# A backward-branch hint on TensorE's inner loop of a GRU recurrence

## The chip, the cores and the metric

The kernel runs on 1 core of one Trainium2 chip. The metric is the device time of one execution in microseconds (us): the median of the runs shown. TensorE is called PE, its weight loads PEld, VectorE DVE, ScalarE ACT, GpSimd POOL and SyncE SP. Each engine has a sequencer that takes instructions in program order, does register work, waits and branches itself, and hands the rest to the engine; the profile writes the sequencer of PE as PEq or PEldq. L340 is line 340 of the kernel.

## The reference

The whole program is one transformer-like layer over x of shape (4, 512, 512): a GRU over the time axis, a causal differential attention with a frequency filter, a second attention, and a mixture of 64 experts with a shared one. Only the GRU bears on the change. With D = 512, B = 4 and T = 512 steps:

```python
def cell(h, x):
    gi = x @ W_ih + b_ih
    gh = h @ W_hh + b_hh
    i_r, i_z, i_n = jnp.split(gi, 3, axis=-1)
    h_r, h_z, h_n = jnp.split(gh, 3, axis=-1)
    r = jax.nn.sigmoid(i_r + h_r)
    z = jax.nn.sigmoid(i_z + h_z)
    n = jnp.tanh(i_n + r * h_n)
    h_new = (1.0 - z) * n + z * h
    return (h_new, h_new)
```

Each step needs the h of the step before, so 512 steps follow one another whatever else is free. All numbers are float32.

## The kernel before

`gru_stage` does the 512 steps. W_hh lies in the tile `ahead`, cut into 4 row chunks (c) and 4 column chunks (j). On PE one step is two functions.

`add_z_input(s, par)` (L296 to L305) waits for the pick of the step from POOL and for two DVE transposes of earlier steps, and then writes the z gate's input into PSUM, 4 products of 32 columns at L300 and 4 of 96 at L304.

`step(s, par)` multiplies h by W_hh, always at L311 in the helper `part`. It waits for the first quarter of h (`h_ready[0]`), multiplies it for the r and z columns (`gru_prz`) and the n columns (`gru_pn`), waits for the rest of h (`h_ready[1]`), and multiplies the other three quarters for `gru_prz`, `gru_pn` and last `gru_pz`. DVE transposes the results (L410, L415, L423), ACT applies sigmoid and tanh, and DVE forms the new h in two scans at L429, which release the next step's `h_ready[0]` and `h_ready[1]`.

For the first 480 steps PE also prepares the recurrence inputs 32 steps ahead: between `add_z_input` and `step` stands `next_gate_input` (L334), one of four 128-row products that make up one column chunk.

The loops on PE are nested. The outer one (L339) runs over 15 blocks of 32 steps, the inner one (L340) over 8 column chunks, and in it 4 steps are written out. So the inner body is run 120 times: 105 times its closing branch is taken, and 15 times it falls through to the branch of the outer loop, which is taken 14 times. The last 32 steps are a loop of their own (L346) with 2 steps in its body and no `next_gate_input`. `Fori` closes each loop with a register add and one compare-and-branch on the line of the loop. The other engines have loops of their own over the same steps (ACT L375 and L376, DVE L441 and L442, POOL L274 and L276), tied to PE by semaphores alone; there is no barrier at a loop's end. Each engine does its work in the order in which it is written.

Of the kernel before, what the change touches and what calls it, by code (L numbers as in the profile page):

```python
# [187 lines left out]
def gru_stage(nc, t, b_hh, next_weights):  # L188
# [8 lines left out]
    with ExitStack() as ctx:  # L197
# [9 lines left out]
        NG, NBL = 2 * KD, T // 32  # L207
# [31 lines left out]
        @block.sync  # L239
        def _(sp):  # L240
            sp.wait_ge(bias_set, 3)
            sp.dma_start(bias[0:1, :, :].rearrange("p j f -> p (j f)"), b_hh[2 * D:3 * D].unsqueeze(0)).then_inc(loaded, 16)

            sp.wait_ge(zero_set, 1)
            R = 16
            yk = t.yk_dram.rearrange("(n r p) d -> n p r d", r=R, p=P)
            for n in range(CHOICES // (R * P)):
                sp.dma_start(yk[n], zeros[:].broadcast_to([P, R, D])).then_inc(cleared, 16)
            sp.wait_ge(cleared, 16 * (CHOICES // (R * P)))

            sp.wait_ge(gi_psum, (NBL - 1) * NG)
            w = t.ahead2[:].rearrange("p (n c f) -> p n c f", n=3, c=KD)
            for n, W in enumerate(next_weights):
                for jj in range(KD):
                    sp.dma_start(w[32 * jj:32 * jj + 32, n, :, :],
                                 W.rearrange("(jj c i) n -> jj i c n", jj=KD, c=KD)[jj]).then_inc(ahead_in, 16)
            sp.wait_ge(ahead_in, 16 * 3 * KD)
# [29 lines left out]
        @block.tensor  # L287
        def _(pe):
            pe.wait_ge(loaded, 16)

            pe.wait_ge(tn_done, 1)
            for j in range(KD):
                last = nc.tensor.matmul(pn[32 * j:32 * j + 32, 0:P], one[:], bias[:, j, :], start=True, stop=True)
            last.then_inc(opened, 1)

            def add_z_input(s, par):  # L296
                pe.wait_ge(pick_ready, s * 1 + 1)
                pe.wait_ge(tr_done, s * 1 + 1)
                for j in range(KD):
                    nc.tensor.matmul(prz[32 * j:32 * j + B, P:P + 32], pick[:, par, :], zin[:, j * P:j * P + 32],  # L300
                                     start=True, stop=True)
                pe.wait_ge(tz_done, s * 1 + 1)
                for j in range(KD):
                    last = nc.tensor.matmul(pz[32 * j:32 * j + B, par, 0:P - 32], pick[:, par, :], zin[:, j * P + 32:(j + 1) * P],  # L304
                                            start=True, stop=True)  # L305
                last.then_inc(z_added, 1)

            def part(rows, of, cols, cs, done=None):
                for c in cs:
                    for j in range(KD):  # L310
                        last = nc.tensor.matmul(rows(j), of(c), whh[:, c, j, cols], start=False, stop=True,  # L311
                                                skip_group_check=True)
                if done is not None:
                    last.then_inc(done, 1)

            def step(s, par):
                after = lambda c: t.h[:, c * B:(c + 1) * B, 6]
                places = lambda c: t.h[:, c * B:(c + 1) * B, :].rearrange("p b x -> p (b x)")
                rz_rows = lambda j: prz[32 * j:32 * j + B, RZ]
                n_of = lambda j: pn[32 * j:32 * j + 32, 0:P]  # L320
                pe.wait_ge(h_ready[0], s * 1 + 1)
                part(rz_rows, after, RZ, (0,))
                pe.wait_ge(seeded, s * 1 + 1)
                part(n_of, places, N, (0,))
                pe.wait_ge(h_ready[1], s * 1 + 1)
                part(rz_rows, after, RZ, (1, 2, 3), r_rows)
                part(n_of, places, N, (1, 2, 3), n_rows)
                part(lambda j: pz[32 * j:32 * j + B, par, 0:P - 32], after, Z, range(KD), z_rows)

            def next_gate_input(kb, c, k):  # L330
                if k == 0:
                    pe.wait_ge(gi_out, kb * NG + c + 1)
                    pe.wait_ge(wst_ready, kb * NG + c + 1)
                last = nc.tensor.matmul(pgi[:, 0:P], wst[:, k, :], xT[:, k, :, bass.ds(kb * 32 + 32, 32)],  # L334
                                        start=(k == 0), stop=(k == KD - 1))
                if k == KD - 1:
                    last.then_inc(gi_psum, 1)

            with pe.Fori(0, NBL - 1) as kb:  # L339
                with pe.Fori(0, NG) as c:  # L340
                    for k in range(KD):
                        s = kb * 32 + c * KD + k
                        add_z_input(s, k % 2)
                        next_gate_input(kb, c, k)
                        step(s, k % 2)
            with pe.Fori(T // 2 - 16, T // 2) as q:  # L346
                for par in range(2):
                    s = q * 2 + par
                    add_z_input(s, par)
                    step(s, par)  # L350
# [2153 lines left out]
```

## Time and profile before

| | |
|---|---|
| median of 3 runs | 3907.85 us |
| lowest and highest | 3906.92 and 3917.58 us |
| the profiled execution's own time | 3908.48 us |
| its span, first to last instruction | 3906.8 us |
| PE busy | 3668.3 us, 94% |
| DVE busy | 2267.9 us, 58% |
| ACT busy | 1507.9 us, 39% |
| mean granted TensorE clock | 0.979 |

Busy times are those of the engine, without the sequencer's own work. An idle time is put down to the instruction on another engine that ended it; "issue" stands where the profile shows nothing that was waited for, so that the engine's own sequencer was late. Matmuls of PE overlap, and the end of each is modelled, so their starts are to be read, not their ends.

### The profile page before, as it was taken

Reading aid. Unit: us, or ns where it says so; the run is one execution under the profiler, and the core shown is the slowest. Engines: PE = TensorE matmul, PEld = TensorE weight load, DVE = VectorE, ACT = ScalarE, POOL = GpSimd, SP = SyncE. Lnnn points to the kernel's source line nnn. Section 1 sums busy time; section 2 is a strip of 40 time slices with the busy share of each in tenths; the row PEclk is TensorE's granted clock in tenths of the full one; section 3 lists DMA queues with packets and bytes.
Section 4 is the critical chain, followed back from the end, with each engine's and each line's share of the span. In section 5 each row is a group of like instructions: output and inputs, shape, how many; then the busy total and the mean of one; then the engine's idle time right before and its main releaser. Section 6 shows DMA issues by size and latency. Waiting matters only on the chain. (4 is left out here: it accounts for less than half of the span.)

```text
span 3906.8 us, 168625 instructions
## 1 busy us (share of the span) xinstructions
PE 3668.3 (94%) x69056; PEld 2363.5 (60%) x69087; DVE 2267.9 (58%) x5855; ACT 1507.9 (39%) x5283; POOL 506.0 (13%) x1077
## 2 busy tenths in 40 slices
PE   7899999999999999999799999968899999889999
PEld 3788888888888888887534444324433333455554
DVE  2566666666666666666477777745366666542228
ACT  0344444444444444444344444532344444321110
POOL 0011111011111110110022222210000000024430
PEclk9999999999999999999899999989999998999999
DMA  4700000000000000001111111102111111159987
GB/s 115 258 0 0 0 0 0 0 0 0 0 0 0 0 0 0 0 0 32 56 39 38 56 38 42 33 10 91 49 50 55 48 55 58 50 172 306 316 249 291
DMA packets 130517, 244.83 MB, mean 63 GB/s; under 512 B 18613, under 2 KB 72129, under 8 KB 126483
## 3 DMA queue, kind: packets, MB, share of 16 engines
q1 hardware_dynamic: 109874, 190.92, 14.5%
q10 hardware_dynamic: 9760, 25.70, 2.3%
q0 software_dynamic: 10816, 27.33, 2.2%
q8 instruction: 41, 0.67, 0.1%
q14 instruction: 26, 0.21, 0.0%
HBM read 147.92 MB, written 50.33 MB: 51 GB/s over the span
## 5 line engine op out<-in xcount | busy, mean ns | idle before, releaser
L311 PE MATMUL gru_prz<-ahead,h 128*4 128x160 f32 x16384 | 747.4, 300 | 9.8 <-DVE h L429 9.8
L311 PE MATMUL gru_pn<-ahead,h 128*32 128x128 f32 x16384 | 635.5, 273 | 0.0
L311 PEld LDWEIGHTS gru_pn<-ahead,h 128*32 128x32 f32 x16384 | 490.0, 110 | 34.7
L311 PEld LDWEIGHTS gru_prz<-ahead,h 128*4 128x4 f32 x16384 | 387.2, 87 | 147.3 <-DVE h L429 20.6
L410 DVE STREAM_TRANSPOSE gru_tr<-gru_prz 128x160 f32<-128x160 f32 x512 | 179.1, 350 | 467.4 <-PE gru_prz L311 467.4
L311 PE MATMUL gru_pz<-ahead,h 128*4 128x96 f32 x16384 | 432.7, 246 | 6.6 <-issue 6.6
L366 ACT ACTIVATE gru_rn<-gru_pre 128x16 f32<-128x16 f32 x512 | 119.7, 234 | 745.6 <-DVE gru_pre L413 745.6
L311 PEld LDWEIGHTS gru_pz<-ahead,h 128*4 128x4 f32 x16384 | 363.1, 87 | 8.5 <-issue 7.3
L943 DVE TENSOR_REDUCE da_mx<-da_ps 128x2 f32<-128x1024 f32 (+3 forms) x256 | 201.3, 817 | 131.8 <-PE da_ps L636 131.8
L272 POOL COPY gru_pick<-ident 128x4 f32 x512 | 96.5, 188 | 1374.1 <-PE gru_pz L304 1368.2
L429 DVE TENSOR_TENSOR_SCAN h<-gru_d 128x16 f32<-128x16 f32 (+1 forms) x1024 | 236.2, 231 | 51.6 <-ACT gru_d L373 0.7
L850 ACT ACTIVATE da_probT<-da_ps 128x1024 f32<-128x1024 f32 (+3 forms) x256 | 169.5, 701 | 193.8 <-PE da_ps L657 191.4
L334 PE MATMUL gru_pgi<-wide,gru_wst 128*128 x960 | 234.4, 326 | 3.9
L334 PEld LDWEIGHTS gru_pgi<-wide,gru_wst 128*128 128x128 f32 x960 | 143.1, 188 | 92.5 <-issue 92.5
L567 POOL TENSOR_SCALAR_AFFINE_SELECT da_probT<-da_probT 128x256 f32<-128x256 f32 x256 | 141.9, 565 | 418.3 <-ACT da_probT L850 418.2
L415 DVE STREAM_TRANSPOSE gru_tn<-gru_pn 128x128 f32<-128x128 f32 x512 | 162.8, 318 | 48.8
L304 PE MATMUL gru_pz<-gru_zin,gru_pick 128*4 128x96 f32 x4096 | 179.5, 247 | 0.0
L360 ACT ACTIVATE gru_rn<-giT 128x16 f32 x512 | 120.4, 235 | 150.3 <-issue 147.4
L1627 DVE TENSOR_REDUCE fa_mx<-fa_ps 128x2 f32<-128x1024 f32 x128 | 150.6, 1218 | 44.6 <-PE fa_ps L1446 44.5
L2115 PE MATMUL ex_pg<-ahead,ex_xT 128*128 128x384 f32 x512 | 175.8, 486 | 0.3 <-DVE ex_xT L2221 0.3
L369 ACT ACTIVATE gru_pn<-gru_bias_rows 128x128 f32<-128x128 f32 x512 | 144.2, 282 | 49.8
L420 DVE TENSOR_TENSOR_SCAN gru_narg<-gru_tn,gru_rn 128x64 f32<-128x64 f32 x512 | 149.4, 292 | 17.5
(314 smaller groups left out, 5699.6 us busy)
## 6 DMA issues: line engine op xcount, KB each, us to landing
ahead<-in_L_ffn_gate_up_proj SPq DMA_DIRECT2D x64, 768.0 KB, 8.1
yk<-gru_zeros SPq DMA_DIRECT2D x6, 4096.0 KB, 31.6
ex_wd<-in_L_ffn_down_proj ACTq DMA_DIRECT2D x64, 384.0 KB, 7.5
ahead<-yk SPq DMA_DIRECT2D x16, 1536.0 KB, 8.7
ahead<-wide SPq DMA_DIRECT2D x15, 1024.0 KB, 4.7
ahead<-xnT SPq DMA_DIRECT2D x15, 1024.0 KB, 4.5
da_wg<-ahead SPq DMA_DIRECT2D x45, 256.0 KB, 4.8
fa_wg<-ahead SPq DMA_DIRECT2D x45, 256.0 KB, 4.7
```

What stands on the lines that cost most here:

```text
L304: last = nc.tensor.matmul(pz[32 * j:32 * j + B, par, 0:P - 32], pick[:, par, :], zin[:, j * P + 32:(j + 1) * P], start=True, stop=True)
L311: last = nc.tensor.matmul(rows(j), of(c), whh[:, c, j, cols], start=False, stop=True, skip_group_check=True)
L334: last = nc.tensor.matmul(pgi[:, 0:P], wst[:, k, :], xT[:, k, :, bass.ds(kb * 32 + 32, 32)], start=(k == 0), stop=(k == KD - 1))
L369: nc.scalar.activation(pn[:, 0:P], bias_rows[:], ACT.Copy).then_inc(seeded, 1)
L410: nc.vector.transpose(tr[:].rearrange("p c x -> p (c x)"), prz[:, RZ]).then_inc(tr_done, 1)
L415: nc.vector.transpose(tn[:], pn[:, 0:P]).then_inc(tn_done, 1)
L420: nc.vector.tensor_tensor_scan(narg[:].rearrange("p c o -> p (c o)"), tn[:, 0:KD * 32:2], rn[:].rearrange("p c o -> p (c o)"), 0.0, ALU.mu ...
L429: nc.vector.tensor_tensor_scan(t.h[:].rearrange("p c x -> p (c x)")[:, part.start * 32:part.stop * 32:2], d0[:, of, :].rearrange("p c o -> ...
L850: nc.scalar.activation(probT[:, n % 2, 2 * part:2 * part + 2, n * P:T], ps[:, KBANK[2 * part]:KBANK[2 * part] + 2, n * P:T], ACT.Exp, scal ...
L943: nc.vector.tensor_reduce(mx[:, i, a, 2 * part:2 * part + 2], ps[:, bank:bank + 2, 0:(i + 1) * P], AX, ALU.max).then_inc(max_done, 1)
L1627: nc.vector.tensor_reduce(mx[:, i, 2 * half:2 * half + 2], ps[:, 2 * half:2 * half + 2, :], AX, ALU.max).then_inc(max_done, 1)
L2115: last = nc.tensor.matmul(pg[:, u % 2, 0:2 * I], xT[:, u % 2, k, :], wg[:, u, k, :], start=(k == 0), stop=(k == KD - 1))
```

## The change

The inner loop is opened with the general form of `Fori`, restricted to PE, with `hint_back_edge=True`. The loop variable, the bounds and the body stay as they are. [...] The compare-and-branch itself stays. The outer loop and the loop of the last 32 steps have no hint.

```diff
             with pe.Fori(0, NBL - 1) as kb:
-                with pe.Fori(0, NG) as c:
+                with nc.Fori(0, NG, engines=[mybir.EngineType.PE], hint_back_edge=True) as c:
                     for k in range(KD):
                         s = kb * 32 + c * KD + k
                         add_z_input(s, k % 2)
```

[...]

## Rows read from the trace of the kernel before

**Rows 1.** The page, busy time of the engines, and the costliest groups of instructions:
```profile
PE 3668.3 (94%) x69056; PEld 2363.5 (60%) x69087; DVE 2267.9 (58%) x5855; ACT 1507.9 (39%) x5283; POOL 506.0 (13%) x1077
...
L311 PE MATMUL gru_prz<-ahead,h 128*4 128x160 f32 x16384 | 747.4, 300 | 9.8 <-DVE h L429 9.8
...
L334 PE MATMUL gru_pgi<-wide,gru_wst 128*128 x960 | 234.4, 326 | 3.9
...
L304 PE MATMUL gru_pz<-gru_zin,gru_pick 128*4 128x96 f32 x4096 | 179.5, 247 | 0.0
```

**Rows 2.** Busy time by stretch, the 480 steps of the inner loop:
```profile
core 0: us, PE busy (x) PEld busy (x) DVE busy (x) ACT busy (x) POOL busy (x), PEclk, DMA share, GB/s
104.40:1791.70 1687.30, 1664.93 (x54724) 1390.60 (x54720) 1024.65 (x3958) 739.21 (x3839) 172.54 (x615) 1.00 0.04 15
```

**Rows 3.** Weight loads in order of time, a step without a branch:
```profile
1018.97 0.71 PEld L311 LDWEIGHTS gru_pz<-ahead,h 128*4 128x4 f32 x32
1019.65 0.19 PEld L300 LDWEIGHTS gru_prz<-gru_zin,gru_pick 128*4 128x4 f32 x8
...
1020.07 0.30 PEld L334 LDWEIGHTS gru_pgi<-wide,gru_wst 128*128 128x128 f32 x2 [0.17 <-issue]
1020.51 0.12 PEld L311 LDWEIGHTS gru_prz<-ahead,h 128*4 128x4 f32 x8
```

**Rows 4.** The same, the next step, which begins behind the inner branch:
```profile
1020.89 0.76 PEld L311 LDWEIGHTS gru_prz<-ahead,h 128*4 128x4 f32 x24
...
1022.37 0.71 PEld L311 LDWEIGHTS gru_pz<-ahead,h 128*4 128x4 f32 x32
1023.36 0.14 PEld L300 LDWEIGHTS gru_prz<-gru_zin,gru_pick 128*4 128x4 f32 x8 [0.29 <-issue]
...
1023.83 0.30 PEld L334 LDWEIGHTS gru_pgi<-wide,gru_wst 128*128 128x128 f32 x2 [0.27 <-issue]
1024.24 0.12 PEld L311 LDWEIGHTS gru_prz<-ahead,h 128*4 128x4 f32 x8
...
1024.63 0.35 PEld L311 LDWEIGHTS gru_prz<-ahead,h 128*4 128x4 f32 x12
```

**Rows 5.** DVE in order of time, the scans that release h:
```profile
1020.26 0.55 DVE L429 TENSOR_TENSOR_SCAN h<-gru_d 128x16 f32<-128x16 f32 x2
...
1023.67 0.54 DVE L429 TENSOR_TENSOR_SCAN h<-gru_d 128x16 f32<-128x16 f32 x2
```

**Rows 6.** PE's sequencer at lines 340 and 298, window 1022 to 1024:
```profile
L340 PEldq ALU_OP  x1: 32/32/32, 1022.7 to 1022.7; - x1
L340 PEldq COMPARE_BRANCH  x1: 207/207/207, 1022.8 to 1022.8; - x1
L340 PEldq FUSED_REGOPS  x1: 128/128/128, 1023.1 to 1023.1; - x1
...
L298 PEldq EVENT_SEMAPHORE  x1: 51/51/51, 1023.3 to 1023.3; - x1
```

**Rows 7.** Weight loads behind an outer branch:
```profile
1009.43 0.14 PEld L300 LDWEIGHTS gru_prz<-gru_zin,gru_pick 128*4 128x4 f32 x8 [0.71 <-issue]
```

**Rows 8.** The sequencers' own instructions over the span, by line of loop:
```profile
L340 PEldq FUSED_REGOPS  x120: 127/128/144, 104.2 to 1777.0; - x120
...
L340 PEldq COMPARE_BRANCH  x120: 76/208/233, 128.5 to 1791.1; - x120
L340 PEldq MOVE  x15: 29/29/37, 104.1 to 1679.6; - x15
...
L346 PEldq COMPARE_BRANCH  x16: 76/208/219, 1797.9 to 1899.9; - x16
```

**Rows 9.** DMA of the core from 300 to 1700 us:
```profile
DMA packets 0, 0.00 MB, mean 0 GB/s; under 512 B 0, under 2 KB 0, under 8 KB 0
```

**Rows 10.** DMA queues of the page, and the instruction queue from 100 to 150 us:
```profile
q8 instruction: 41, 0.67, 0.1%
...
q8 instruction: 4, 0.07, 0.5%
```

## Prediction

> **What bounds the kernel now.** I read the page first. PE is busy 94% of the span, and its costliest group is the product at L311 [rows 1]. The busy time by stretch shows that the 480 steps of the inner loop take 1687.3 us with PE at full granted clock, which is 43% of the 3906.8 us span [rows 2]. The recurrence is serial, so anything that makes one of the 120 iterations of L340 longer is added 120 times, and the rest of the program (2219.5 us) isn't touched by the diff.
>
> The mean of a stretch doesn't say whether the branch matters. For that I laid weight loads in order of time beside the scans that release h. In a step without a branch, loads follow one another without a gap from `gru_pz` at 1018.97 to L300 at 1019.65, 0.68 us later [rows 3]. The scans end at 1020.26 + 0.55 = 1020.81, and the first load that needs all of h starts at 1020.89, 0.08 later [rows 4, 5]. There PE waits for h, and a little sequencer time on PE would be hidden.
>
> Behind the inner branch it is the other way round. `gru_pz` begins at 1022.37 and L300 at 1023.36, 0.99 us later instead of 0.68, with 0.29 us of idle put down to issue [rows 4]. The scans end at 1023.67 + 0.54 = 1024.21, so with the same 0.08 the load could start at 1024.29; it starts at 1024.63 [rows 4, 5]. PE is 0.34 us late there, and not because of h. In starts of L300, the three steps up to 1019.65 take (1019.65 - 1009.43)/3 = 3.41 us each, the step over the branch 1023.36 - 1019.65 = 3.71 [rows 3, 4, 7]. So a back edge costs some 0.30 us today, about 0.3 x 105 = 31 us in all. Behind an outer branch the idle before L300 is 0.71 us instead of 0.29 [rows 7].
>
> What fills it is visible on the sequencer: a register add of 32 ns at 1022.7, the compare-and-branch of 207 ns, a register operation of 128 ns, a wait of 51 ns, then the load at 1023.36 [rows 4, 6]. These are 418 ns of the 660 between 1022.7 and 1023.36, so about 240/4 = 60 ns lie behind each. I take it as a rule of this trace that an instruction of PE's sequencer occupies its duration plus 60 ns.
>
> **The change, part by part.**
>
> *The hint, added.* One more sequencer instruction at the top of each of 120 iterations, right behind the branch and ahead of the register operation at L340. That is the place where PE is already late by 0.34 us, both behind an inner branch and, more so, behind an outer one, so nothing hides it. The delay runs on: L300, L334, the first L311 loads, then the rest stand in program order [rows 4], and h, the next step and DVE, ACT and POOL wait behind them by semaphores. No later step gives it back, since each begins with the h that came late. No trace row shows the instruction itself. Its lower end is the cheapest register move at L340, 29 + 60 = 89 ns; the upper end of the likely stretch is the register operation there, 128 + 60 = 188 ns [rows 8]. [...] I take 0.14 us. Ends: 120 x 0.089 = 10.7 us, 120 x 0.188 = 22.6 us; taken value 120 x 0.14 = 16.8 us.
>
> *The branch, hinted.* The compare-and-branch stays. What could the hint save on it? A taken one is 208 ns, one that falls through 76 [rows 8], so at most 132 ns x 105 = 13.9 us, if a hinted branch were as cheap as one not taken. Against it: the loop at L346 has half the steps and no L334 in its body, and its taken branches are 208 ns as well [rows 8]. The duration doesn't follow the distance jumped, and looks like the fixed work of changing the place of fetching. I take a saving of nothing, and keep 13.9 us for the range.
>
> *Code that must be fetched.* This is what a hint would be for, and whether there is anything to save is the heart of the case. The body is long: 54,724 matmuls and 54,720 loads in 480 steps are 228 instructions per step, 912 per iteration, beside the waits [rows 2]. If its start had to be fetched anew at each back edge there would be packets on the instruction queue. Between 300 and 1700 us, which is some 100 iterations, the core moved no DMA packet of any kind [rows 9]. The whole program has 41 packets on that queue [rows 10], fewer than the 120 iterations of this loop alone. The whole body stays where the sequencer can reach it. So nothing is saved here: 0.
>
> [...]
>
> *Leaving the loop.* If the hint makes the sequencer prepare for the loop's start and not for the code behind it, the exit may pay one fetch. On the instruction queue 4 packets take 0.5% of 16 engines x 50 us, 1.0 us each [rows 10]. Once: 0 to 2 us, I take 0. The loads before and after the recurrence are unchanged, and one more instruction ahead of them shifts code only.
>
> **Sum.** +16.8 us on the profiled execution's 3908.48 us gives 3925.3. That execution is 0.63 us over the median of the runs, 3907.85, so the predicted median is 3924.7, 0.43% slower.
>
> **Rivals.**
>
> *Something of the back edge goes (faster).* The mechanism: the sequencer refills from the branch's target without a packet that the profile sees, and the hint starts this refill early. Price: at best all of the 0.30 us excess of an inner back edge disappears, -31 us over 105 edges, against the hint's own 120 x 0.089 = 10.7: net -21, 3887. It decides where the saving per edge is over 0.10 us more than the hint costs. For it: 0.29 us of issue idle are there to be had [rows 4]. Against it: the rows account for that idle with four ordinary instructions, and no row shows a fetch. Chance 0.06. [...]
>
> *The branch itself becomes cheap.* A hinted branch of 76 instead of 208 ns: -13.9 + 10.7 = -3 us, 3905; with a dearer hint up to +9 us. For it: PE's taken branch is 132 ns longer than its other one. Against it: the same 208 in the short loop [rows 8]. Chance 0.08, all but 0.01 of it within the noise.
>
> *The hint does nothing and costs nothing*, because it is dropped or lies where the queued loads of `gru_pz` cover it: 3908. For it: loads of `gru_pz` are still queued when the branch starts (1022.37 + 0.71 = 1023.08 against 1022.8) [rows 4, 6]. Against it: that cover is used up 0.29 us before L300 starts. Chance 0.07.
>
> *The hint is heavy.* It takes as long as the taken branch, 208 + 60 = 268 ns: 120 x 0.268 = 32 us, 3940. [...] Chance 0.06.
>
> *The hint triggers a fetch each time*, of code that is already there: 120 more packets of 1.0 us. If the sequencer waits for each, +120 to +140 us, 4040. Against it: nothing but that the code is resident. Chance 0.03.
>
> **How the numbers follow.** My case, a hint of 89 to 188 ns fully exposed, has 0.70. About 0.3% is what a measurement of this kernel can tell from no change: 11.7 us, or 98 ns per iteration. That cuts off the cheapest tenth of my stretch and, as a plain register move is a real possibility, I give 0.19 of the 0.70 to within 0.3% and 0.51 to slower. Slower: 0.51 + 0.06 + 0.03 = 0.60. Within: 0.19 + 0.07 + 0.07 = 0.33. Faster: 0.06 + 0.01 = 0.07. The range reaches from 3906 (nothing, or a cheaper branch) to 3938 (almost the heavy hint); the fetch, the large gain and the tail of the heavy case are left out. My own case alone is 3918.5 to 3930.5.
>
> **What would show it.** In the changed kernel's sequencer rows, 120 new instructions at the line of the inner loop, with a duration between 29 and 128 ns. The compare-and-branch at L340 still 208 ns taken. The idle before L300 behind an inner branch up from 0.29 to about 0.43, the step over the branch from 3.71 to 3.85 us, plain steps still 3.41. The 480 steps 1704 us instead of 1687.3. Still no packet from 300 to 1700 us. The forecast is wrong if the step over the branch gets shorter, if the branch's duration falls, or if the queue of instructions has over a hundred packets more.

## The result, and the profile after

Over 13 runs of each kernel the changed one takes 3920.99 us (3916.25 to 3921.81) against 3910.16 us (3906.49 to 3917.58); the medians are 10.8 us apart. The ratio, taken over all these runs, is 1.0023, with a 95% interval of 1.0014 to 1.0032: slower by some 9 us, with an interval that excludes no change, but inside the 0.3% that I had called the limit. Beside the experiments it was timed again (e1) at 1.0032 (1.0020 to 1.0043), just outside that limit. The profiled execution has a span of 3914.5 us against 3906.8.

First the busy time of the 480 steps, the stretch that answers to [rows 2]:

```profile
105.40:1803.90 1698.50, 1666.64 (x54721) 1391.99 (x54721) 1020.92 (x3958) 738.21 (x3838) 172.59 (x615) 1.00 0.04 15
```

They take 1698.5 us instead of 1687.3, 11.2 us more, with PE at the same granted clock of 1.00. The rest of this one execution took 3.5 us less, 2216.0 against 2219.5. It has no line of the change; the clock was granted differently there, 0.982 over the span against 0.979. So the stage is the place to read the change from, not the span.

Then the sequencer of PE at the inner loop, over the span [rows 8]. The columns are the duration in ns (least, median, most) and the first and last start:

```profile
L340 PEldq BRANCH_PREFETCH_HINT  x120: 31/31/50, 105.0 to 1789.0; - x120
L340 PEldq FUSED_REGOPS  x120: 127/128/144, 105.1 to 1789.1; - x120
L340 PEldq ALU_OP  x120: 32/32/32, 129.6 to 1803.1; - x120
L340 PEldq COMPARE_BRANCH  x120: 80/223/258, 129.7 to 1803.2; - x120
```

The hint is there 120 times, at the top of the iteration ahead of the register operation (105.0 against 105.1 us in the first), and lasts 31 ns, almost the register move of 29 ns. The register operation behind it starts 89 ns after it. The compare-and-branch has a median of 223 ns instead of 208. Last, the weight loads over an inner branch, which answer to [rows 4]:

```profile
1029.35 0.71 PEld L311 LDWEIGHTS gru_pz<-ahead,h 128*4 128x4 f32 x32
1030.40 0.14 PEld L300 LDWEIGHTS gru_prz<-gru_zin,gru_pick 128*4 128x4 f32 x8 [0.35 <-issue]
...
1031.29 0.12 PEld L311 LDWEIGHTS gru_prz<-ahead,h 128*4 128x4 f32 x8
1031.68 0.76 PEld L311 LDWEIGHTS gru_prz<-ahead,h 128*4 128x4 f32 x24
```

From `gru_pz` to L300 it is 1.05 us instead of 0.99, and from one group of `gru_prz` loads to the next (1027.88 before these rows) 3.80 us instead of 3.74. These single edges show too little: the one of rows 4 is among 12 of 98 whose step takes 3.74 us, where most take 3.69. The medians from `gru_pz` to L300 over all inner edges are 0.95 and 1.06 us. For a measure that uses all edges I took the time from the start of each scan that completes h at L429 to the next one. Its median is 3.400 us in the three plain steps of both kernels, and over the branch 3.691 us before and 3.791 after. Over an outer edge it is 4.15 and 4.22. So 105 inner edges lose 0.100 us each and 14 outer ones 0.07, 11.5 us together, which agrees with the 11.2 of the stretch. Between 300 and 1700 us one packet of instructions moved, before none [rows 9].

### The profile page after: what moved, and what is told of

The parts are those of the page before. It is cut to its first block and busy times, and to the rows that moved or that the text cites. A ratio compares the mean times of both kernels' runs of the same rounds, so it can differ in the third digit from the quotient of the medians.

```text
span 3914.5 us, 168745 instructions
## 1 busy us (share of the span) xinstructions
PE 3666.7 (94%) x69056; PEld 2363.9 (60%) x69087; DVE 2263.4 (58%) x5855; ACT 1507.2 (39%) x5283; POOL 507.5 (13%) x1077
## 5 line engine op out<-in xcount | busy, mean ns | idle before, releaser
L311 PE MATMUL gru_prz<-ahead,h 128*4 128x160 f32 x16384 | 747.9, 300 | 9.7 <-DVE h L429 9.7
L311 PE MATMUL gru_pn<-ahead,h 128*32 128x128 f32 x16384 | 636.6, 273 | 0.0
L311 PEld LDWEIGHTS gru_pn<-ahead,h 128*32 128x32 f32 x16384 | 491.0, 110 | 35.3
L311 PEld LDWEIGHTS gru_prz<-ahead,h 128*4 128x4 f32 x16384 | 387.1, 87 | 146.9 <-DVE h L429 20.3
L311 PE MATMUL gru_pz<-ahead,h 128*4 128x96 f32 x16384 | 433.2, 246 | 4.8 <-issue 4.8
L311 PEld LDWEIGHTS gru_pz<-ahead,h 128*4 128x4 f32 x16384 | 363.5, 87 | 6.8 <-issue 5.5
L429 DVE TENSOR_TENSOR_SCAN h<-gru_d 128x16 f32<-128x16 f32 (+1 forms) x1024 | 233.9, 228 | 52.5 <-ACT gru_d L373 0.8
```

Of the source, the lines that this page charges most:

```text
L429: nc.vector.tensor_tensor_scan(t.h[:].rearrange("p c x -> p (c x)")[:, part.start * 32:part.stop * 32:2], d0[:, of, :].rearrange("p c o -> ...
```

## Experiments

Theory A: a hint is one more sequencer instruction at a point of PE that has no cover, and as all code of the loop is at hand, it has nothing to save. Theory B: the hint costs by what it does to the fetching of code. In later runs C, D and E name theories on where code stays. Step times over an edge are medians of the time between scans of h, as above. e1 to e4, e5 to e8 and e9 to e12 were timed in three sets, each with the kernel before beside it (3909.40, 3909.66 and 3911.63 us), and the ratios are to these. Unless said otherwise an edit is against the kernel before. A kernel with more steps in the body covers the same 480 steps in fewer iterations; nothing is left out in any of them.

**e1, the changed kernel again.**

> The changed kernel again, to have its time beside the others on one chip. Theory A (a hint is one more sequencer instruction on a path with no cover, and saves nothing): 9 to 13 us over the kernel before, the step over the inner branch 100 ns longer (89 ns of slot and some 11 ns of a dearer branch). Theory B (the hint costs through what it does to the fetching of code, not through its place): the same time, since this is the run to be explained.

3922.79 us, ratio 1.0032 (1.0020 to 1.0043); the step over the inner branch 3.788 us. As A says. One row differs from the first profile of this same kernel, the branch, with a median of 216 ns and not 223:

```profile
L340 PEldq COMPARE_BRANCH  x120: 80/216/257, 129.6 to 1802.9; - x120
```

**e2, something else in the hint's place** (the edit is against the changed kernel).

```diff
-                with nc.Fori(0, NG, engines=[mybir.EngineType.PE], hint_back_edge=True) as c:
+                with pe.Fori(0, NG) as c:
+                    pe.wait_ge(opened, 1)
```

> No hint; in its place, as the first instruction of each iteration on PE, a wait on a semaphore that has long been met. Theory A: any sequencer instruction costs its slot there. A met wait lasts 51 ns, with the gap of about 55 some 106 ns, x120 = +12.7 us; step over the inner branch 3.691 to 3.797 us; the compare-and-branch stays at 208 ns. Theory B: without the hint the cost is gone, under +3 us.

3919.72 us, ratio 1.0021 (1.0012 to 1.0031). The wait did not become the instruction that I expected. The rows of PE's sequencer show what came in its stead, 120 more register moves and the register operation, now under L297 with 108 ns:

```profile
L340 PEldq MOVE  x135: 29/29/38, 103.1 to 1788.3; - x135
L340 PEldq ALU_OP  x120: 32/32/32, 128.1 to 1802.3; - x120
L340 PEldq COMPARE_BRANCH  x120: 83/215/229, 128.2 to 1802.4; - x120
```
```profile
L297 PEldq FUSED_REGOPS  x120: 107/108/124, 103.6 to 1788.4; - x120
```

A plain register move of 29 ns per iteration stands where the hint of 31 ns stood. The instruction behind it starts 88 ns after the move, and 89 after the hint: at this place the two take the same slot. There is no hint, and the recurrence takes about as long as in the changed kernel, 11.0 us more than before against 10.2. The step over the inner branch has a median of 3.807 us and a mean of 3.788, against means of 3.793 in the changed kernel and 3.697 before. B falls for at least the larger part of the cost.

The sum is not as clean as that. The register operation behind the move is 20 ns shorter than before, so the sequencer reaches L300 only 75 ns later than in the kernel before (603 against 528 ns after the branch's start), and not 104 as in the changed kernel (632). Of 98 inner edges 41 lose these 75 ns (3.76 us); at the others another 47 ns go between L300 and L311 (3.81 us). I don't know what takes them.

The branch's duration here is 215 ns without any hint, and so it is in e9, whose loop wasn't edited at all. With e1's 216 for the hinted kernel, a dearer branch is not shown to come from the hint.

**e3, the hint where loads are queued.**

```diff
                 part(rz_rows, after, RZ, (1, 2, 3), r_rows)
+                if mark:
+                    marked.append(pe.mark_branch_hint_location())
...
+                        step(s, k % 2, mark=(k == KD - 1))
+                    nc.regs_alu(regs, regs, 1, op=mybir.AluOpType.add)
+                    pe.br_lt(regs, NG, on_true="late_loop", on_false="late_end").branch_hint(marked.pop())
```

> The hint is moved from the top of the iteration into its fourth step, behind the loads of the three last quarters of h for gru_prz, where PE's array is behind its sequencer. Theory A: the 89 ns are hidden, only the 11 to 15 ns by which the hinted compare-and-branch is longer stay: +1.3 to +1.8 us, within noise of the kernel before; step over the inner branch about 3.705 us. Theory B: as the changed kernel, +9 to +13 us, since the hint does the same wherever it stands.

3915.18 us, ratio 1.0013 (1.0004 to 1.0022); the step over the branch 3.707 us. The same 120 hints are there:

```profile
L330 PEldq BRANCH_PREFETCH_HINT  x120: 31/31/50, 123.3 to 1791.9; - x120
```

Of the 0.100 us per edge 0.084 are gone in the median, since the hint stands where PE's array is behind: the next loads in program order, those of `gru_pn`, start 0.66 us after the hint in the median. What stays is 0.016 us, with a branch of 216 ns. That makes 2 us, a little over the 1.3 to 1.8 that I expected. The recurrence took 2.8 us more than before in the profile, because 33 of 98 inner edges take 3.75 us and not 3.70, for a reason as unknown as e2's 47 ns. The timed +5 us (1.6 to 8.6) has its lower end near this, and I don't know what the rest is. On place against presence the run is clear.

**e4 and e5, twice the body, without and with the hint.**

```diff
-                with pe.Fori(0, NG) as c:
+                with pe.Fori(0, NG // 2) as g:
+                    for cc in range(2):
+                        c = g * 2 + cc
...
```

(e5 has `nc.Fori(0, NG // 2, engines=[mybir.EngineType.PE], hint_back_edge=True)` for the loop over g.)

> No hint; PE's inner loop has 8 steps in its body instead of 4, so 4 iterations per block instead of 8 and 45 taken inner branches instead of 105. Theory A (the whole cost of a back edge is sequencer time behind the branch, the body is resident): 60 edges of 0.291 us fewer, -17.5 us, 0.45% faster, still next to no instruction packets between 300 and 1700 us. Theory B (fetching matters): the body is twice as long, about 1824 loads and matmuls and the waits, so a fetch at each back edge: over a hundred more packets on the instruction queue and a time not below that of before.

> The body of 8 steps with the hint. In the run without it the taken inner branch lasted 3.3 to 3.9 us, and 538 instruction packets fell into the recurrence, 9 per iteration. Theory A (a hint pays exactly where a taken branch waits for code): the branch falls to some 0.22 us and 45 inner edges save 3.4 us or more each, -150 us or better against e4, to 4090 or less; outer branches, without a hint, stay at 3.3 to 3.9 us. Theory C (with all of the body gone from the store, the wait only moves to the next piece of code): 4200 to 4250 and about as many packets.

e4: 4246.24 us, ratio 1.0858 (1.0839 to 1.0877). Theory A had the fastest kernel so far and it is the slowest; with this body fetching matters, as B had it. e5: 3920.82 us, ratio 1.0025 (1.0015 to 1.0035). One hint per iteration is worth 325 us here. The branch rows and the instruction queue from 300 to 1700 us, e4:

```profile
L340 PEldq COMPARE_BRANCH  x60: 76/3544/7080, 152.2 to 2122.1; - x60
```
```profile
L339 PEldq COMPARE_BRANCH  x15: 67/3642/3886, 262.0 to 2122.3; - x15
```
```profile
q8 instruction: 380, 6.23, 1.9%
```

and e5:

```profile
L340 PEldq BRANCH_PREFETCH_HINT  x60: 31/31/50, 104.1 to 1763.1; - x60
L340 PEldq COMPARE_BRANCH  x60: 87/228/261, 152.2 to 1790.9; - x60
```
```profile
L339 PEldq COMPARE_BRANCH  x15: 72/214/214, 235.6 to 1791.2; - x15
```

Between 300 and 1700 us e5 moved no DMA packet of any kind.

The reader is to see three things. A taken branch lasts 3.6 us in the median in e4, where 380 instruction packets come in between 300 and 1700 us, against 0.2 in e5, where none does: this is what a fetch looks like in this loop. In e4 some 540 instruction packets fall into the recurrence, 9 per iteration of 60. And in e5 not just the branch is short: there is no packet at all, so the whole body of 8 steps stays, and there is room for it. Even the outer branches, which have no hint in e5 and which I had expected at 3.3 to 3.9 us, are short. So the hint didn't hide a fetch, as my theory A had it: with it there was none, 0 packets against 380. My reading is that without a hint the piece behind the loop is fetched ahead, takes a place and drives out what comes next. No row names the piece that a packet carries, so this reading is not shown.

Only part of e4's loss is the branch itself: 59 taken long branches, 3.5 us longer in the mean, are 204 us of some 330. The step over an inner edge is 9.2 us in the mean, 5.8 more than a plain step. Most of what remains is the clock. From 2.6 to 5.7 us after the branch's start, with PE's array idle for some 3.8 us before its first load, the granted clock falls from 1.00 to 0.50, behind 56 of the 59 long branches, and stays there for 3.4 or 6.8 us (17.1 once, behind the first). In the step behind such a pause the same loads take nearly twice as long as in the next step, here 1.30 us and 0.76 us:

```profile
1026.20 0.14 PEld L300 LDWEIGHTS gru_prz<-gru_zin,gru_pick 128*4 128x4 f32 x8 [3.76 <-issue]
...
1028.20 1.30 PEld L311 LDWEIGHTS gru_prz<-ahead,h 128*4 128x4 f32 x24
...
1032.15 0.76 PEld L311 LDWEIGHTS gru_prz<-ahead,h 128*4 128x4 f32 x24
```

Over the whole stretch the granted clock is 0.92:

```profile
104.00:2130.00 2026.00, 1788.84 (x54875) 1467.94 (x54875) 1020.86 (x3970) 741.24 (x3850) 173.06 (x616) 0.92 0.06 17
```

**e6, the body of 8 placed at the start of a piece of code, no hint** (the edit is against e4).

```diff
-                with pe.Fori(0, NG // 2) as g:
+                with nc.Fori(0, NG // 2, engines=[mybir.EngineType.PE], head_slot={mybir.EngineType.PE: 0}) as g:
```

> The body of 8 steps, no hint, the loop's first instruction placed at the start of a 16 KB piece of code. Theory A with a fixed store: e4 fetched 9 packets per iteration, so the body touches one piece more than can stay; 1850 instructions beginning at a piece's start touch one less. If that is all, inner edges are resident and the time is near 3895. Theory D (what is fetched ahead behind the branch also takes a place): still 8 to 9 packets per iteration and a time near 4240, because the piece behind the loop is fetched each time and drives out the first one.

4281.87 us, ratio 1.0964 (1.0931 to 1.0996), 326 packets between 300 and 1700 us, 470 in the recurrence.

```profile
L340 PEldq COMPARE_BRANCH  x75: 76/3370/5015, 103.9 to 2152.4; - x75
```

Placing the body at a piece's start did not make the inner edges resident, as the theory of a fixed store would have it. But D is not borne out in full either. The mean of 7.8 packets per iteration mixes two kinds: 9 of 60 iterations have no packet, a branch of 0.23 us and a step over the edge of 3.7 us, all without a hint, and nearly all others have 9 or 10. What decides between them is open. The run is slower than e4 for a reason of its own: the placed loop is entered by one more taken branch in each block (the 15 rows over the 60 of e4), and the step over an outer edge is 13.5 us instead of 9.6.

**e7, one flat loop of 8 steps, placed, with the hint; e8, one flat loop of 4 steps without a hint.**

```diff
-            with pe.Fori(0, NBL - 1) as kb:
-                with pe.Fori(0, NG) as c:
+            with nc.Fori(0, (NBL - 1) * NG // 1, engines=[mybir.EngineType.PE]) as m:
...
-                pe.wait_ge(gi_out, kb * NG + c + 1)
+                pe.wait_ge(gi_out, m * 1 + cc + 1)
```

(e8's edit; in e7 2 stands for the 1, with `head_slot` and `hint_back_edge=True`. The block's number is computed as `m // (NG // n)`.)

> PE's two loops over the 480 steps are one loop of 60 iterations with 8 steps in the body, its start placed at the start of a piece of code, with the hint. Theory D: the hint turns the fetching ahead from the piece behind the loop to the loop's start, which is there, so nothing is driven out: under 20 packets between 300 and 1700 us, 60 edges at (0.291 + 0.1) us and no outer edges: 1687.3 - 120 x 0.291 - 15 x 0.58 + 60 x 0.39 = 1667 us for the 480 steps, a time of about 3890, 0.5% faster than before. Theory C: packets at each edge and a time above 4000.

> PE's two loops are one loop of 120 iterations with 4 steps in the body, no hint. Theory A: an outer edge costs the next step 4.26 us against 3.69 over an inner one, so 14 outer edges turned into inner ones save 14 x 0.57 = 8 us, less what a dearer register operation at the top costs (the block number is now computed): 3902 to 3908. A rival says that the register work is put at the top of each iteration, at 90 ns and more: +10 us or more less the 8, at or above the time of before.

e7: 3911.24 us, ratio 1.0004 (0.9995 to 1.0014), no packets between 300 and 1700 us, the step over the edge 3.786 us. That is not the 3890 that I expected. Once running, an iteration takes 27.60 us, which makes 1656 us for the 480 steps, but up to the first scan behind the loop it took 1682. e8: 3894.09 us, ratio 0.9962 (0.9948 to 0.9976), the first kernel that beats the one before, and below the 3902 to 3908 that I expected. Its rows say that it gains more than the outer edges:

```profile
L339 PEldq FUSED_REGOPS  x120: 49/50/55, 103.2 to 1761.4; - x120
L339 PEldq ALU_OP  x120: 32/32/32, 128.1 to 1775.2; - x120
L339 PEldq COMPARE_BRANCH  x120: 76/208/229, 128.2 to 1775.3; - x120
```

The register operation at the top fell from 128 to 50 ns, and the step over the edge from 3.691 to 3.610, the same 0.08 us. It is A once more, with the sign turned: a ns of sequencer time there is about a ns of the recurrence. My rival for e8, dearer register work at the top, was wrong.

Some 21 of e7's 26 us went at the start. Its first eight steps took 4.1, 7.9, 5.4, 7.9, 5.4, 8.1, 5.6 and 3.8 us. The kernel before has this too, in its first four: 5.1, 7.0, 7.1 and 4.0 us. In its weight loads:

```profile
112.01 0.20 PEld L311 LDWEIGHTS gru_pz<-ahead,h 128*4 128x4 f32 x4
113.80 0.51 PEld L311 LDWEIGHTS gru_pz<-ahead,h 128*4 128x4 f32 x26 [1.58 <-issue]
...
121.11 0.28 PEld L311 LDWEIGHTS gru_pz<-ahead,h 128*4 128x4 f32 x16 [3.67 <-issue]
```

PE stops in the middle of a group that has no wait in it, and goes on 1.6 or 3.7 us later. In the kernel before a packet of code begins at 111.5, at 118.7 and at 126.1 us and takes 0.9 us each; PE goes on 1.4 to 1.5 us after the first two have ended. The DMA queues from 100 to 150 us have a zero fill of `yk` running, at 98.4% of all 16 engines, and the code's few packets beside it:

```profile
q1 hardware_dynamic: 8922, 18.14, 98.4%
```

The other 5 us of e7 went behind the loop, where the code of the last 32 steps comes in, again in the middle of a group without a wait:

```profile
1786.46 0.44 PEld L311 LDWEIGHTS gru_pz<-ahead,h 128*4 128x4 f32 x17
1791.96 0.27 PEld L311 LDWEIGHTS gru_pz<-ahead,h 128*4 128x4 f32 x12 [5.05 <-issue]
```

From the last scan of the 480 steps to the end of the recurrence it is 108.8 us in the kernel before and in the changed one, and 119.0 in e7. In e5 it is 118.0, and in e4, without a hint, 116.5. So a body of 8 steps pays 8 to 10 us once, on the way out, hint or not.

**e9 to e12, the zero fill later, and the best loops.**

```diff
             sp.wait_ge(zero_set, 1)
+            sp.wait_ge(gi_psum, 2 * NG)
             R = 16
```

> The kernel before with one more wait on SP: the zero fill of yk (6 transfers of 4 MB, landing up to some 150 us) starts after 64 steps of the recurrence. Theory E (the first pass through the loop waits for code whose packets stand behind the zero fill): the first four steps, which took 10.6 us more than 3.4 us each, lose most of that; 6 to 10 us faster, 3900 to 3904. Rival: the first steps are slow for another cause (POOL's copies, a cold start), and the time stays at 3909.

> One loop of 120 iterations with 4 steps, no hint (as e8), and the zero fill later. Theory E: e8's 3894 less the 6 to 10 us of the first pass: 3884 to 3888. Rival of E: 3894.

> One loop of 60 iterations with 8 steps, its start placed at the start of a piece of code, the hint in the body's seventh step where loads are queued, and the zero fill later. Theory A: the hint's 89 ns disappear from the step over the edge, 3.79 to 3.70 us, so an iteration takes 8 x 3.40 + 0.30 = 27.5 us and the 480 steps 1650 + the first pass; with theory E the first pass loses under 8 us instead of the 21 of e7. Time 3911 - 5 - 13 = 3893 or less; if the first pass is as good as in the kernel of 4 steps, 3880. No packets between 300 and 1700 us beyond one or two. If the hint stands too late for the fetching ahead, packets at each edge and a time above 4000.

> The same with 16 steps in the body and 30 iterations: 3,700 instructions, more than the 1,850 that were seen to stay. Theory A says that now every piece is fetched in every iteration, 15 packets each, over 350 between 300 and 1700 us; inside the body the fetching ahead hid them in e4 (steps of 3.40 us), and with the hint the first piece is fetched ahead too. So the edges cost some 0.3 to 0.5 us x 30 and the time is 3870 to 3895. Rival: one piece fetched ahead is not enough over the edge, the second piece is waited for, and the edge costs 3 us or more: above 3970.

e9: 3898.82 us, ratio 0.9974 (0.9965 to 0.9983). The first four steps take 3.4, 3.4, 3.4 and 3.7 us; the recurrence is 8.8 us shorter and the edges stay at 3.692. Theory E holds: with the fill gone the packets of the first pass begin 4 to 5 us apart (107.3, 112.1, 116.0) instead of 7, and PE no longer waits. The same place as above is now one unbroken group (the lines of this kernel are one further down):

```profile
111.74 0.71 PEld L312 LDWEIGHTS gru_pz<-ahead,h 128*4 128x4 f32 x32
```

e10: 3887.43 us, ratio 0.9945 (0.9931 to 0.9959), as the sum of e8 and e9 says.

e11: 3884.56 us, ratio 0.9934 (0.9920 to 0.9947), in the expected range. All first steps are 3.40 us, and the step over the edge is 3.686 us, 0.10 less than in e7: with eight steps in the body and a late hint no instruction packet came between 300 and 1700 us. Against e10's edges of 3.61 it still costs something, 0.02 us at 23 of 59 edges (3.63) and 0.08 at most others (3.69). e10 and e11 beat both kernels. Their intervals overlap, so which of the two is faster isn't settled. The profiles show why they are so near: from the first to the 480th scan of h e11 takes 1646.4 us and e10 1656.1 (before: 1682.0), but from there to the end of the recurrence e11 takes 116.5 us and e10 108.8. What the longer body saves at the edges it mostly pays back on leaving.

e12: 3994.30 us, ratio 1.0216 (1.0202 to 1.0230). The rival that I wrote down for it had the size right:

```profile
L357 PEldq COMPARE_BRANCH  x30: 88/2057/5562, 161.8 to 1865.5; - x30
```
```profile
q8 instruction: 355, 5.82, 1.7%
```

A body of 16 steps does not stay, 15 packets are fetched per iteration, and with the hint the branch still takes 2.1 us in the median and the step over it 7.2. The rival's mechanism, a wait for a second piece, is not what the rows show: PE pauses once, at the branch, and behind it works for a while at the lower clock, as in e4 (0.50 for 3.4 us behind 18 of the 29 taken branches and for 6.8 behind one; 24 loads at L312 take 1.26 us instead of 0.76). Fetching inside the body is hidden (plain steps 3.40 us); over the edge it isn't, even with the hint. No run of 16 steps without a hint was made, so what the hint saves there is open.

## Why the prediction was right and where it was off

**The measured time lies in my range and on the side that I forecast**, 3921 against 3924.7. But I had given 0.60 to slower by over 0.3% and 0.33 to within, and the ratio is 1.0023, within, if barely (e1 has 1.0032). Both the share of that case and the size of the one term behind it were too high.

- *What bounds.* Right. That PE is late behind the branch by its own sequencer carried the whole forecast. e2 and e8 show it with other instructions: a register move in the hint's place takes the same slot, and 78 ns less of register work gives back 81 ns per edge. e3 shows the other side, that the same hint costs next to nothing, 0.016 us per edge, when it stands 1.8 us ahead of the branch.
- *The hint, added.* This is the mis-sized term. I took 0.14 us, about the middle between 89 and 188 ns, an estimate that no run shows; the runs showed 89 ns in its place. The hint lasts 31 ns, and the next instruction starts 89 ns after it: my lower end to the ns. So 120 x 0.089 = 10.7 us and not 16.8. The rule "duration plus 60 ns" held here, with some luck. At the one edge that I read, the branch was followed by 105 ns and the wait by 24, and only their mean with the others was near 60. Over all edges it is 65 ns behind the register add, 58 behind the branch, the register operation and the hint, and 25 behind the wait. What failed was the step from there to 0.14 us. The nearest row was the move, and I should have stayed with it, the more so as the class of the result hung on 98 ns.
- *The branch, hinted.* I took a saving of nothing, and there is none. In the first profile it is 15 ns dearer, 1.6 us over 105 edges, but 8 in the second profile of the same kernel (e1), and unhinted branches reach 215 ns too (e2, e9). The hinted branches of e3, e5 and e7 last 216, 228 and 227 ns. Whether the hint makes a branch dearer at all is open.
- *Code that must be fetched.* Right, and the central point. The 0 packets between 300 and 1700 us told that there was nothing to save. What I missed is how near the edge was: twice the body, and the same hint is worth 325 us. I had reasoned that the body fits; e4 and e6 show that a body which does stay with a hint (e5) can be fetched anew in nearly every iteration without one (9 packets each). My reading, that the piece fetched ahead needs a place as well, was not shown. With the hint 1,850 instructions loop without a packet (e5), and 3,700 move 355 packets between 300 and 1700 us (e12).
- *Leaving the loop.* Nothing measurable: from the last scan of the 480 steps to the end of the recurrence it is 108.8 us in both kernels. A body of 8 steps does pay on leaving, and more than my 0 to 2 us: 8 to 10 us in e4, e5, e7 and e11. It is not the hint that does it, as I had argued there, since e4 has none.
- *The rivals.* All five stand refuted: no part of the idle behind the branch was the hint's to take away, the branch did not become cheap, the hint was neither dropped nor covered, it was not as heavy as a branch, and it triggered no packets (41 on that queue in both kernels).

## What to carry to other kernels

A branch hint is a sequencer instruction with a price of its own, here 0.09 us: before adding one, look for instruction packets during the loop and for taken branches of several us (3.6 us in e4); with neither, it saved nothing here. When a body comes near the size at which code is fetched anew (without a hint 912 loads and matmuls moved no packet here, and twice as many moved 9 per iteration), put the hint in the last part of the body where loads or products are queued (e3: 0.016 us per edge left of 0.100). Lengthening the body was not shown to pay here: e11 saved 10 us at its fewer edges against e10 and lost 8 of them behind the loop. And where an engine is late behind its back edge, first cut what its sequencer does there: the register work at the top (78 ns of it less gave 0.08 us per edge in e8), the second loop level (an outer edge took 4.15 us, an inner one 3.69), and large transfers that run while the body's code comes in for the first time (e9: 8.8 us).

## What was not expected of the hardware

- A loop can fetch code anew in every iteration although there is room for it. With 8 steps in the body and no hint the 60 iterations fetched 9 packets of 16 KB each (0.67 MB / 41, rows 10); with one hint per iteration, none once running. The placed body of e6 fetched none in 9 iterations and 9 or 10 in nearly all others.
- A taken branch on PE mostly lasts 207 to 228 ns with its target at hand and 3.3 to 3.9 us without (e4, with one of 7.1; 2.8 to 5.0 in e6), and the duration stands in the profile at the branch itself.
- Packets of code come later beside a bulk transfer, some 7 us apart and without it 4 to 5: under a zero fill at 98.4% of the DMA engines 16 steps from the first scan on took 10.6 us more than 3.40 each, and with the fill moved 1.3 us, nearly all of it the four edges.
- A pause of PE's array costs twice: after the 3.8 us at a long branch the granted clock fell from 1.00 to 0.50 for 3.4 or 6.8 us (e4), and the next step's work was slower too (24 loads in 1.30 us and not 0.76).
